# Two ScalarE work items cut into pieces (layer-norm statistics, final SiLU), and fewer DMA semaphores, in an eight-core attention and FFN layer

## What is computed

```python
xn = layernorm(x)
q, k = l2norm(proj(xn, Wq)), l2norm(proj(xn, Wk)); v = proj(xn, Wv)
attn = softmax(q @ k.T + alibi + mask)      # key positions 0..127 ahead of the query
s = (attn @ v) @ Wo.T
gate, up = xn @ wg.T, xn @ wu.T             # int32 weights times 1/127, 3072 wide
g = silu((silu(gate) * up) @ wd.T)
return x + s * g
```

## Time and profile before

| | us |
|---|---|
| time, median of two runs | 4507.91 |
| the two runs | 4352.33 and 4663.5 |
| the profiled execution | 4349.8 |
| its span on the slowest core (core 6) | 4348.3 |
| spans of all cores | 4324.8 to 4348.3 |
| TensorE busy | 3472.2 (80% of the span) |
| ScalarE busy | 1954.7 (45%) |
| VectorE busy | 1223.0 (28%) |
| mean granted TensorE clock on core 6 | 0.928 of full |

### The profile page before, as it was taken

The page is one execution under the profiler, slowest core; times in us unless marked ns, Lnnn a source line. Parts: engine busy times, 40 slices in busy tenths (PEclk is TensorE's granted clock), DMA queues, the critical chain, the costliest instruction groups (busy, mean ns, idle before and its releaser), DMA issues.

```text
span 4348.3 us, 59920 instructions; the slowest of 8 cores (4324.8 to 4348.3 us)
## 1 busy us (share of the span) xinstructions
PE 3472.2 (80%) x20160; PEld 1661.7 (38%) x20160; DVE 1223.0 (28%) x2246; ACT 1954.7 (45%) x2875; POOL 131.8 (3%) x292
## 2 busy tenths in 40 slices
PE   2523578888888898888888898888878898889887
PEld 1312333443434343443434343444434343444443
DVE  0101122324233232324233233323232332324141
ACT  4314421635445363635445363635445362635351
POOL 1101000000000000000000000000000000000000
PEclk6656789999999999999999999999999999999999
DMA  5667634434343434334343435344344435334342
GB/s 137 150 153 150 126 123 154 133 125 157 124 145 126 153 117 166 130 126 155 124 155 122 148 119 177 117 134 154 121 155 127 138 119 178 119 122 158 107 151 90
DMA packets 276420, 596.39 MB, mean 137 GB/s; under 512 B 71072, under 2 KB 71072, under 8 KB 258720
## 3 DMA queue, kind: packets, MB, share of 16 engines
q1 hardware_dynamic: 236192, 464.63, 33.1%
q0 software_dynamic: 39936, 127.94, 10.5%
HBM read 558.92 MB, written 60.82 MB: 143 GB/s over the span
## 4 chain that ended last, share of the span: by engine, by line
PE 54%; DMA 15%; ACT 12%; issue 9%; DVE 9%; SPq 0%; POOL 0%; DVEq 0%; ACTq 0%; POOLq 0%
PE psB L520 11%; PE psB L537 10%; PE psA L497 8%; PE psA L563 7%; PE psB L563 6%; PE psA L689 5%; DMA WA<-wdT_s 4%; PE psA L609 3%; DVE STAT L455 3%; DMA WGU<-wgT_s 2%; DVE GBUF L582 2%; ACT GBUF L578 2%; ACT GBUF L384 2%; ACT GBUF L380 2%; DMA wdT_s<-HID 1%
## 5 line engine op out<-in xcount | busy, mean ns | idle before, releaser
L497 PE MATMUL psA<-WA,XN 128*128 128x512 bf16 x3072 | 749.0, 405 | 296.0 <-DVE TM L465 159.8
L537 PE MATMUL psB<-XN,WGU 128*128 128x512 bf16 x3072 | 730.3, 381 | 37.5 <-ACT GBUF L578 29.7
L520 PE MATMUL psB<-XN,WGU 128*128 128x512 bf16 x3072 | 731.3, 381 | 19.0 <-DMA WGU<-wgT_s 15.0
L497 PEld LDWEIGHTS psA<-WA,XN 128*128 128x128 bf16 x3072 | 311.6, 103 | 724.7 <-issue 419.4
L545 DVE TENSOR_TENSOR HID<-psB,TSC 128x512 bf16<-128x512 f32 x384 | 262.8, 691 | 805.2 <-PE psB L537 445.8
L537 PEld LDWEIGHTS psB<-XN,WGU 128*128 128x128 bf16 x3072 | 299.8, 98 | 409.5 <-issue 56.4
L520 PEld LDWEIGHTS psB<-XN,WGU 128*128 128x128 bf16 x3072 | 284.4, 98 | 354.4 <-issue 36.8
L578 ACT ACTIVATE GBUF<-psA,CST 128x1024 f32<-128x1024 f32 x32 | 35.6, 1114 | 817.5 <-PE psB L563 772.4
L627 DVE TENSOR_TENSOR PT<-PT,EB 128x512 bf16<-128x512 bf16 x496 | 211.0, 426 | 590.5 <-ACT PT L622 567.4
L528 ACT ACTIVATE TSC<-psB,CST 128x512 bf16<-128x512 f32 x384 | 259.3, 686 | 256.3 <-PE psB L520 254.2
L582 DVE TENSOR_TENSOR GBUF<-GBUF,SBS 128x1024 f32<-128x1024 f32 x64 | 78.4, 1226 | 897.2 <-ACT GBUF L578 897.2
(11 more groups left out here) (88 smaller groups left out, 2732.4 us busy)
## 6 DMA issues: line engine op xcount, KB each, us to landing
WGU<-wgT_s SPq DMA_DIRECT2D x384, 256.0 KB, 2.7
WGU<-wuT_s SPq DMA_DIRECT2D x384, 256.0 KB, 2.7
WD<-wdT_s SPq DMA_DIRECT2D x96, 512.0 KB, 4.5
WA<-wdT_s SPq DMA_DIRECT2D x96, 512.0 KB, 3.9
XL<-x POOLq DMA_DIRECT2D x16, 2048.0 KB, 10.7
WA<-wkT_s SPq DMA_DIRECT2D x32, 1024.0 KB, 7.1
WA<-wvT_s SPq DMA_DIRECT2D x32, 1024.0 KB, 6.9
XE<-x POOLq DMA_DIRECT2D x16, 2048.0 KB, 9.8
```

What stands on the lines that cost most here:

```text
L497: last = e.matmul(psA[:, 512 * tc:512 * tc + 512], XN[p1][:, 512 * dc + 128 * tc:512 * dc + 128 * tc + 128], wap[:, 512 * dc:512 * dc + 51 ...
L520: last = e.matmul(psB[:, go:go + 512], gap[:, goff + 128 * dc:goff + 128 * dc + 128], XN[p][:, 512 * dc:512 * dc + 512], start=(dc == 0), ...
L537: last = e.matmul(psB[:, uo:uo + 512], uap[:, uoff + 128 * dc:uoff + 128 * dc + 128], XN[p][:, 512 * dc:512 * dc + 512], start=(dc == 0), ...
```

## The change

Three edits:

- NDMASEM goes from 8 to 6, for both queues.
- `ln_stats` is cut into `ln_stats_tc(gt, tc)` (Copy and Square of one row group) and `ln_stats_fin(gt)` (the POOL chain, root and reciprocal). In a tile, row groups 0 and 1 stay where all four stood; groups 2 and 3 and `ln_stats_fin` go behind the v projection, ahead of the first attention block.
- The SiLU of the epilogue is cut into two instructions of 512 columns, one for each PSUM bank, both into GBUF. The VectorE operations behind it stay whole.

```diff
-NDMASEM = 8
+NDMASEM = 6
...
-        def ln_stats(gt):
-            for tc in range(TCN):
-                xsl = XL[:, 1024 * tc:1024 * (tc + 1)]
...
+        def ln_stats_tc(gt, tc):
+            xsl = XL[:, 1024 * tc:1024 * (tc + 1)]
+            P.op("act", (lambda e, xsl=xsl, tc=tc: e.activation(
+                GBUF[:, :], xsl, AF.Copy,
+                accum_out=st(LNS4 + tc))),
+                reads=[bXL], writes=[bG, bLN1], tag=f"lnsum{gt}_{tc}")
+            P.op("act", (lambda e, xsl=xsl, tc=tc: e.activation(
+                GBUF[:, :], xsl, AF.Square,
+                accum_out=st(LNSS4 + tc))),
+                reads=[bXL], writes=[bG, bLN1], tag=f"lnss{gt}_{tc}")
+
+        def ln_stats_fin(gt):
             P.op("gp", lambda e: e.tensor_scalar_mul(
...
-            P.op("act", (lambda e, pt=pt, off=off: e.activation(
-                GBUF[:, :], pt[:, off:off + 1024], AF.Silu, scale=CST[:, 2:3])),
-                reads=[bp[2 * (tc % 2)], bp[2 * (tc % 2) + 1], bCST],
-                writes=[bG], tag=f"gsilu{g}_{tc}")
+            for hh in range(2):
+                P.op("act", (lambda e, pt=pt, off=off, hh=hh: e.activation(
+                    GBUF[:, 512 * hh:512 * hh + 512],
+                    pt[:, off + 512 * hh:off + 512 * hh + 512],
+                    AF.Silu, scale=CST[:, 2:3])),
+                    reads=[bp[2 * (tc % 2) + hh], bCST],
+                    writes=[bG], tag=f"gsilu{g}_{tc}_{hh}")
...
             if has_ln:
-                ln_stats(g + 2)
+                ln_stats_tc(g + 2, 0)
+                ln_stats_tc(g + 2, 1)
...
+            if has_ln:
+                ln_stats_tc(g + 2, 2)
+                ln_stats_tc(g + 2, 3)
+                ln_stats_fin(g + 2)
+
             nwq0 = load_wa("wq", 0, f"wq0_{g + 1}") if g + 1 < n_iters else None
```

More of the change, by code:

```diff
@@ L836, in build_nc @@
         load_x(0, "ldx0")
-        ln_stats(0)
+        for _tc in range(TCN):
+            ln_stats_tc(0, _tc)
+        ln_stats_fin(0)
         ln_apply(0)
@@ L840, in build_nc @@
         load_x(1, "ldx1")
-        ln_stats(1)
+        for _tc in range(TCN):
+            ln_stats_tc(1, _tc)
+        ln_stats_fin(1)
         ln_apply(1)
```

## The result

| | before | changed |
|---|---|---|
| median of all runs, us | 4497.47 (10 runs) | 4411.61 (11 runs) |
| lowest, us | 4337.48 | 4403.65 |
| ratio of comparable runs, 95% interval | 1 | 1.0122 (1.0093 to 1.015) |
| profiled execution, us | 4349.8 | 4408.76 |
| spans of the cores, us (mean) | 4324.8 to 4348.3 (4336.2) | 4382.3 to 4407.2 (4395.9) |

The changed kernel is 1.2% slower, and its interval excludes no change. The medians stand the other way round only because in some executions of either kernel the cores of one die ran at a lower clock, more often in the runs of before; the ratio leaves those out. From profile to profile the change costs 59 us, where 47 were forecast.

What follows compares the result with a forecast made beforehand. TensorE mostly sets the pace, losing most to normalization waits behind ScalarE and VectorE. Statistics 22, tile 0 3, SiLU 22 and semaphores 0 sum to +47 us on 4349.8: 4397 us, range 4350 to 4425.

Steps and rivals of the forecast that it cites:

- The two numbers: Whole kernel: forecast time 4397 us, 1.1% above the profiled 4349.8, and range 4350 to 4425 us.
- The chances: Whole kernel against a 2% resolution: faster by over 2% 0.03, slower by over 2% 0.10, the rest 0.87.
- the covered lump: Rival in attention: later blocks take up the late exponentials, leaving -6.8 us in 13 tiles; 4284 us, chance 0.06.
- k projection: Two row groups of statistics leave it: L465 ends 6.8 us earlier, TensorE stands 0.4 us instead of 7.3.
- The stall in attention: First block, tiles 1 to 13: second q-k product waits 6.2 us for late exponentials; with clock 8.5 (6.5 to 9.25).
- The clock's share: Half clock behind the new wait in attention costs 2.3 us of full-speed work, up to 3.05.
- The rival in which the clock stays full: In attention, no clock drop behind the 6.2 us wait: +21 us, 4371 us; chance 0.12.
- Tile 0: No gain ahead of its attention; a 5.49 us store wait there takes most of the added 8.3: +3 us (0 to +8).
- SiLU halves: Epilogue: a pair takes 1.46 us instead of 1.11, 1.39 us a tile, 22 us in all (0 to 26).
- Semaphores: DMA queues with six instead of eight: the sixth load before has landed, so 0 us.
- Table loads: 13 or so more at L459, inside the 4.44 us from square to L465's end; the skill's drain would add 18 us.

Runs made afterwards that it cites:

- c_ln2: Kernel before with only the statistics cut in two, their second part ahead of attention; ratio 1.0078 (1.0046 to 1.011).
- e_root_late: As c_ln2, but the statistics' root and its table load wait until behind the attention blocks; ratio 1.0077 (1.0029 to 1.0126).
- f2_cover: As c_ln2, but in tiles 1 to 13 one FFN unit moved from tile end between the first block's two q-k products; ratio 1.005 (1.0033 to 1.0068).
- m_tile0: As c_ln2, but in tile 0 alone all statistics and their POOL chain stand ahead of the k projection again; ratio 1.0083 (1.0053 to 1.0113).
- d_silu2n: Kernel before with the epilogue's SiLU in two halves, each with its own buffer name; profiled 4596.23 us at granted clock 0.85 to 0.87, no ratio.

## Why the prediction was right or wrong, point by point

- **The two numbers.** 4397 us (1.1% above the profiled 4349.8) lies inside the measured ratio's interval, and 4350 to 4425 held the time.
- **The chances: wrong.** The sum gave the time; the step from the sum to an outcome failed. It is "a measurement of this kernel can tell about 2% from no change". The comparison resolved 0.3% either way, so that 1.2% (1.0093 to 1.015) was a clear loss. Of the cases that I had weighed, only the covered lump, at 0.06, was quicker than before; all others were slower. With that, "within 2%" at 0.87 said too little, and the outcome to name was slower. I took the 311 us between the two runs shown for the scatter of a measurement, although one of them agreed with the profiled execution within 3 us.
- **k projection: right.** L465 was to be 6.8 us earlier; to the last copy k is 7.0 us shorter (7.1 in c_ln2), the wait 0.56 us (0.4 forecast).
- **The stall in attention: right.** 6.2 us forecast, 6.0 to 6.3 measured; with the clock 8.5, measured 8.9. The clock's share was 2.8 us, not 2.3, inside its range (to 3.05). The rival in which the clock stays full fell, and e_root_late and f2_cover showed that stalls of 2.6 to 2.9 us are followed by half clock too, in 190 of 208 cases.
- **The new lump is covered: wrong rival.** Later blocks are 62.1 us in every kernel of the table; they gave nothing back.
- **Tile 0: the term that was mis-sized.** "+3 us (0 to +8)" was 12 (14 in c_ln2, and m_tile0 took 14 back). I had followed ScalarE's queue and not POOL's. The chain of the statistics is moved past POOL's load issues too, and this is where the time went. Nine of the 12 us between 47 and 59 are here; the other three are no more than cores and executions differ by. That the whole time came within 12 us is thus no sign that this term was understood.
- **SiLU halves: right.** +1.4 us a tile forecast and measured; d_silu2n splits it in two about equal parts. The first bank was free 0.43 us sooner, as worked out, and the restart waited longer for it.
- **Semaphores: right**, 0.
- **Table loads.** 13 more at L460 (58, 45 before), as forecast. Two loads of different sets stand at 2085.99 and 2087.51 of the changed kernel, each 1.28 us with the next instruction some 0.02 us behind it. The drain of 1380 ns that the Trainium skill gives for a switch ("ScalarE: Activation LUTs", "What ACT_TABLE_LOAD costs") does not show in this trace, and 4415 us by that page lies near the measured time for a reason that the trace does not bear out.

## What to carry to other kernels

Work on an in-order engine that was moved here from one waiting place to another only moved the stall, and added a table load; look for a stage in which that engine pauses between instructions, and deal the work out one piece to a pause. Splitting an instruction to free its bank sooner brings nothing where the next one waits for a shared scratch buffer: a second buffer gave 4.2 us a tile, the split took 1.4. When a step is moved, follow each queue that it passes, the one that only issues transfers too: it may have been holding back transfers that get in the way elsewhere.

## What the runs showed of the hardware

A TensorE stall of 2.62 us was in 86 of 104 cases followed by matmuls at 1.2 GHz (in one of them a granted clock of 0.66 over ten microseconds, and eight gate matmuls in 3.59 us instead of 1.9); I had expected this for 6 us and left it open for 3. The trace of before could have told: its down projection stalls 2.76 us in tile 6, and the first four matmuls take 1.87 us where four later ones take 1.03.

```profile
2145.32 1.87 PE L563 MATMUL psA<-WD,HID 128*128 128x512 bf16 x4 [2.76 <-ACT XN L440]
...
2148.47 1.03 PE L563 MATMUL psA<-WD,HID 128*128 128x512 bf16 x4
```

Three 256 KB stores that wait for each other took 6.4 us alone (6.42 before, 6.35 in m_tile0), from the first issue to the third, and 14.5 to 16.6 us beside GpSimd's loads of gate and up weights (int32 in the source, bf16 in the buffer).
